# Who scales the raw expert weights in the weight preparation: GpSimd or ScalarE

## The reference

```python
# attention: 16 heads of 16, causal, only the 32 largest scores of each row kept
scores = where(causal, -inf, q @ k.T / 4); keep the top 32 of each row; softmax; @ v; @ Wo.T + bo
# experts: 8 experts, all computed for every token, weighted by a gate
h = relu(einsum('edi,bsi->bsed', proj_in, x))        # proj_in  8 x 512 x 256
o = einsum('eid,bsed->bsei', proj_out, h)            # proj_out 8 x 256 x 512
gate = einsum('bks,bkse->bse', weights, one_hot(ensembles, 8)); out = einsum('bsei,bse->bsi', o, gate)
# feed-forward: Hadamard transform, 4-bit activations, ternary weight
```

## Time and profile before

| | us |
|---|---|
| median of 3 runs | 622.53 |
| the profiled execution, its own time | 624.53 |
| its span in the trace | 622.7 |
| PE busy | 553.3 (89%) |
| DVE busy | 477.5 (77%) |
| ACT busy | 387.2 (62%) |
| POOL busy | 344.3 (55%) |
| DMA queue of the loads and stores | 9.6% of the 16 engines' span |

### The profile page before, as it was taken

The page is one execution under the profiler, slowest core; times in us unless marked ns, Lnnn a source line. Parts: engine busy times, 40 slices in busy tenths (PEclk is TensorE's granted clock), DMA queues, the critical chain, the costliest instruction groups (busy, mean ns, idle before and its releaser), DMA issues. The chain is left out here.

```text
span 622.7 us, 20334 instructions
## 1 busy us (share of the span) xinstructions
PE 553.3 (89%) x7156; PEld 478.9 (77%) x7156; DVE 477.5 (77%) x2995; ACT 387.2 (62%) x909; POOL 344.3 (55%) x336
## 2 busy tenths in 40 slices
PE   4565648999899999999999999999999999989942
PEld 3454537898788888888888888888888888878831
DVE  1898879986889978898879887988789898553213
ACT  3688558666567566766667576766575767646520
POOL 2488556753447464754556455655554656555831
PEclk9568578999999999999999999999999999999985
DMA  7244220001000200002000100020001000000000
GB/s 234 78 146 136 86 103 2 3 17 37 3 2 3 64 8 2 3 3 69 3 1 21 53 3 2 3 70 1 3 3 53 3 3 1 19 0 3 18 0 17
DMA packets 20021, 19.88 MB, mean 32 GB/s; under 512 B 1744, under 2 KB 17872, under 8 KB 19920
## 3 DMA queue, kind: packets, MB, share of 16 engines
q1 hardware_dynamic: 19920, 18.59, 9.6%
HBM read 16.49 MB, written 2.10 MB: 30 GB/s over the span
## 5 line engine op out<-in xcount | busy, mean ns | idle before, releaser
L462 POOL TENSOR_TENSOR h_lo<-h_raw,h_hi 128x512 f16<-128x512 f32 x128 | 149.5, 1169 | 158.9 <-ACT h_raw L580 158.2
L768 PE MATMUL ps_o<-w_hi,h_lo 128*128 128x256 f16 x512 | 139.8, 273 | 4.3 <-POOL h_lo L462 3.1
L752 PE MATMUL ps_z<-x1t_hi,w_lo 128*128 128x256 f16 x512 | 140.5, 274 | 0.6 <-DVE x1t_lo L910 0.6
L752 PE MATMUL ps_z<-x1t_lo,w_hi 128*128 128x256 f16 x512 | 140.3, 274 | 0.0
L752 PE MATMUL ps_z<-x1t_hi,w_hi 128*128 128x256 f16 x512 | 140.3, 274 | 0.0
L768 PE MATMUL ps_o<-w_hi,h_hi 128*128 128x256 f16 x512 | 139.5, 273 | 0.0
L768 PE MATMUL ps_o<-w_lo,h_hi 128*128 128x256 f16 x512 | 139.5, 273 | 0.0
L854 DVE MATCH_REPLACE8 taken<-next,taken 128x48 f32<-128x48 f32 (+2 forms) x576 | 127.6, 233 | 0.2
L576 ACT ACTIVATE h_hi<-ps_z 128x512 f16<-128x512 f32 x128 | 75.9, 593 | 57.9 <-PE ps_z L752 57.0
L849 DVE MAX8 next<-taken 128x8 f32<-128x48 f32 (+2 forms) x576 | 95.9, 235 | 0.1
L483 POOL TENSOR_TENSOR acc<-go_sb,acc 128x512 f32<-128x512 f32 x56 | 71.2, 1271 | 36.4 <-ACT go_sb L590 36.2
(11 more groups left out here) (106 smaller groups left out, 993.5 us busy)
## 6 DMA issues: line engine op xcount, KB each, us to landing
w_raw<-in_w1t SPq DMA_DIRECT2D x8, 512.0 KB, 3.8
w_raw<-in_w2t SPq DMA_DIRECT2D x8, 512.0 KB, 5.0
xt_sb<-in_xt SPq DMA_DIRECT2D x8, 256.0 KB, 3.3
x_sb<-in_x SPq DMA_DIRECT2D x8, 256.0 KB, 3.1
out<-out_sb SPq DMA_DIRECT2D x8, 256.0 KB, 2.1
ctx_sb<-in_ctx_w SPq DMA_DIRECT2D x8, 128.0 KB, 2.3
itok_sb<-in_itok SPq DMA_DIRECT2D x8, 128.0 KB, 2.5
wq_sb<-in_wqt SPq DMA_DIRECT2D x1, 256.0 KB, 2.9
```

Of the source, the lines that this page charges most:

```text
L462: nc.gpsimd.tensor_tensor(h_lo[:, e % 2, 2 * z:2 * z + 2, :], h_raw[:, z, :, :], h_hi[:, e % 2, 2 * z:2 * z + 2, :], ALU.subtract)\
L752: last = pe.matmul(ps_z[z][:, d * UT:(d + 1) * UT], w[:, e, c, at:at + P], x[:, c, :], start=n == 0, stop=n == len(terms) - 1)
L768: last = pe.matmul(ps_o[e % 2][:, b * D:(b + 1) * D], h[:, e % 2, c, b * SEQ:(b + 1) * SEQ], w[:, e, c, :], start=n == 0, stop=n == len(te ...
```

## The change

ACT makes the scaled raw array too: after each high part it runs a second activation over the same raw array, with the same scale, that writes the float32 result in place. The semaphore that GpSimd waits for is now raised by this second activation. GpSimd's scaling instruction and its wait are gone; its subtraction stays. For each expert ACT issues four 128x1024 activations instead of two, and GpSimd two instructions of that size instead of four. Nothing is moved in the order of the steps, and w2's high part now stands behind w1's scaling.

```diff
                 elif name in ("w1_low", "w2_low"):
                     e, = args
-                    i, raw, hi, lo, step_done, ready = (
-                        (0, w1_raw, w1_hi, w1_lo, w1_low_step, w1_low_ready) if name == "w1_low" else
-                        (1, w2_raw, w2_hi, w2_lo, w2_low_step, w2_low_ready))
+                    i, raw, hi, lo, ready = ((0, w1_raw, w1_hi, w1_lo, w1_low_ready) if name == "w1_low" else
+                                             (1, w2_raw, w2_hi, w2_lo, w2_low_ready))
                     pool.wait_ge(w_high_ready, 2 * e + i + 1)
-                    nc.gpsimd.tensor_scalar(raw[:, e % STAGED, :, :], raw[:, e % STAGED, :, :],
-                                            w_pow[:, e, i:i + 1], 1.0, ALU.mult, ALU.mult).then_inc(step_done, 1)
-                    pool.wait_ge(step_done, e + 1)
                     nc.gpsimd.tensor_tensor(lo[:, e, :, :], raw[:, e % STAGED, :, :], hi[:, e, :, :],
                                             ALU.subtract).then_inc(ready, 1)
...
                 elif name == "w_high":
                     e, = args
                     act.wait_ge(w_step, 3 * (e + 1))
-                    act.activation(w1_hi[:, e, :, :], w1_raw[:, e % STAGED, :, :], ACT.Copy,
-                                   scale=w_pow[:, e, 0:1]).then_inc(w_high_ready, 1)
-                    act.activation(w2_hi[:, e, :, :], w2_raw[:, e % STAGED, :, :], ACT.Copy,
-                                   scale=w_pow[:, e, 1:2]).then_inc(w_high_ready, 1)
+                    for i, (raw, hi) in enumerate(((w1_raw, w1_hi), (w2_raw, w2_hi))):
+                        act.activation(hi[:, e, :, :], raw[:, e % STAGED, :, :], ACT.Copy, scale=w_pow[:, e, i:i + 1])
+                        act.activation(raw[:, e % STAGED, :, :], raw[:, e % STAGED, :, :], ACT.Copy,
+                                       scale=w_pow[:, e, i:i + 1]).then_inc(w_high_ready, 1)
```

## The result

The changed kernel takes 630.07 us (median of 4 runs, 629.77 to 632.81) against 622.68 us before (4 runs): 7.4 us more. The profiled execution took 630.36 us with a span of 628.6 us, 5.8 and 5.9 us more than the one of before. Forecast were 6.4 more and 628.9 us.

What follows compares the result with a forecast made beforehand. PE bounds 200 to 580 us; before 94 us an engine-to-engine chain does. Terms 3.1 + 0 + 2.0 - 1.6 + 0.8 + 0.9 + 1.2 = 6.4 us on 622.53 give 628.9 us, range 624.9 to 631.4.

Steps and rivals of the forecast that it cites:

- Price of the added work: ACT's queue: each expert's two added float32 activations cost 2.1 us, bounds 0 and 2.3.
- Tile 0, 3.1: w_high 0 and 1 ahead of copy_scores and second copy_probs: keep 1.0 us late, attend and normalise 3.1 late.
- Tile 1, hidden: w_high 2: ACT's 2.03 us idle before the next copy hides the added 2.1; lateness stays 3.1.
- Tile 2, plus 2.0: w_high 3 straight before the exponentials that keep already waited for: no cover, plus 2.0, lateness 5.1.
- Tile 3, minus 1.6 plus 0.8: DVE's wait and slow small steps at w_scale(4) give back 1.6; w_high 4 makes keep wait 0.8; lateness 4.3.
- From keep of tile 3 to the first layer norm, lateness kept: Through turn_probs, copy_probs, attend and normalise the chain stays 4.3 us late; time won on DVE is worth nothing.
- w_high(5), costed at nothing: Expert 5's added activations hide in ACT's wait for PE's v product; uncovered they would cost 2.1 us.
- First layer norm, plus 0.9: ln1_apply's first DVE instruction is held by a subtraction, 2.1 us instead of 1.1; plus 0.9, lateness 5.2.
- Rival 1: Layer norm race goes otherwise: DVE slips in, 627.2 us, or w_high(6) is too late for POOL, 625.4; chance 0.22.
- Expert 7, plus 1.2: w_high 7 before exp(1|1): keep 1.2 us late, so PE's scores of tile 1|3 wait 1.2 more.
- Rival 3, the clock: Between 94 and 112 us PE's low-clock stretch is as long again: 2.0 us more, 630.9; chance 0.13.
- Rivals 2 and 4: 2: ACT's idle time hides everything, 622.5 us, chance 0.08. 4: the freed POOL/DVE port makes it faster, 619.1, chance 0.04.

Runs made afterwards that it cites:

- the kernel with expert 7 behind: Against the kernel before: ACT scales only expert 7, after exp and relu, and GpSimd's low parts of expert 7 move down its order; ratio 1.0013.
- the five experts: Against the kernel before: ACT's second, scaling activations only for experts 0, 1, 3, 4 and 7, GpSimd scaling the others; 630.16 us, ratio 1.0117.
- the single test: Against the kernel before: ACT's second, scaling activations only for experts 0 and 1, GpSimd scaling the others; ratio 1.0050, 3.1 us more.
- the fourth experiment: Kernel before plus one wait: GpSimd starts expert 6's low parts only when x1 is written, away from ln1_apply; 626.63 us, ratio 1.0071.
- the single ones: Three kernels against the one before: ACT scales only experts 0 and 1, only 3 and 4, or only 7; ratios 1.0050, 1.0056, 1.0026.
- the trace with expert 6 on ACT: Against the kernel before: ACT scales only expert 6, and GpSimd starts its low parts after the ternary weights are done; 621.72 us, ratio 0.9976.
- the one with the wait alone: Against the kernel before: GpSimd still scales every expert, but starts expert 6 only after the ternary weights are done; 626.77 us, ratio 1.0062.
- all scaling moved behind: Against the kernel before: all 16 scaling activations on ACT as a separate step, behind the exponentials or in an ACT wait; 638.01 us, ratio 1.0253.

## Why the prediction was right

The time lies in the forecast range, and the mechanism, place by place, was right up to tile 3. But that the sum fits so well is partly luck. Forecast were 6.4 us; measured are 7.4 by medians, 5.9 between the profiled executions and 8.4 (6.7 to 10.0) by the ratio of the runs, which leaves 6.4 just outside. In the two profiled executions errors of both signs cancel, and the reason is the clock during tile 3. The rows: PE's v product before, ACT's copy of v before and after, and the v product in the kernel with expert 7 behind, whose code is that of before up to there:

```profile
73.73 3.78 PE L645 MATMUL ps_misc<-wv_sb,xt_sb 128*128 128x256 f32 x8 [0.64 <-DVE o_sb L874]
...
77.55 0.60 ACT L525 ACTIVATE v_sb<-ps_misc 128x512 f32<-128x512 f32 x1 [2.99 <-PE ps_misc L645]
```

```profile
79.64 0.58 ACT L521 ACTIVATE v_sb<-ps_misc 128x512 f32<-128x512 f32 x1
```

```profile
73.93 2.00 PE L654 MATMUL ps_misc<-wv_sb,xt_sb 128*128 128x256 f32 x8 [0.64 <-DVE o_sb L883]
```

Seven traces have unchanged code up to here. Counted from the first w_squares, keep of tile 3 begins at 48.8 to 49.1 us in all of them. Then v takes 3.5 to 3.8 us in four (the kernel before among them) and 2.0 in three, and ln1_apply begins at 71.1 to 71.9 us in the first and 69.0 to 69.3 in the others. So traces have to be compared with traces of the same level. The changed kernel ran v at the upper level. All positions in us from the first w_squares:

| experts scaled by ACT | first w_squares at | keep of tile 3 | ln1_apply | first expert product | scores of 1\|3 | end of the span |
|---|---|---|---|---|---|---|
| *v at the lower level:* none (before) | 16.25 | 48.9 | 71.7 | 77.8 | 91.9 | 606.5 |
| 0, 1, 3, 4, 7 | 17.12 | 53.0 | 75.7 | 81.8 | 97.1 | 612.0 |
| 3, 4 | 17.02 | 50.0 | 72.7 | 78.8 | 92.9 | 607.4 |
| *v at the upper level:* 7, behind exp | 17.19 | 49.0 | 69.0 | 75.1 | 89.1 | 603.6 |
| 0, 1 | 15.85 | 51.8 | 72.2 | 78.3 | 92.4 | 606.9 |
| 2, 5, 6 | 16.42 | 48.8 | 70.8 | 77.6 | 91.1 | 605.6 |
| all (changed) | 15.56 | 53.5 | 74.6 | 81.5 | 97.1 | 613.0 |

At the lower level the five experts end 5.5 us later than the kernel before, which is the sum of the prediction's terms for them (6.4 less the 0.9 of the layer norm). At the upper level the changed kernel ends 9.4 us later than the one with expert 7 behind: 3 us more than forecast. This is one trace of each kernel, but the 8.4 us of the runs lie beside it. Term by term:

- **Price of the added work:** right, 1133 ns and a next start at 2 x 2.1 us. (Eight times 2.1 is 16.8, not 16.9; the sum doesn't use it.)
- **Tile 0, 3.1:** right. Keep waits 1.08 us for ACT at 28.25, normalise waits 3.11 instead of 1.03, and the single test gives 3.1 us by times and 3.2 by the table.
- **Tile 1, hidden:** right; keep of tile 1 shows no wait.
- **Tile 2, plus 2.0:** right, the keep's wait went from 0.52 to 2.49.
- **Tile 3, minus 1.6 plus 0.8:** nearly. w_scale(4) no longer waits and its small steps take 0.17 us; keep is 3.9 late, 4.6 counted from the first w_squares, against 4.3. Alone, experts 3 and 4 make keep 1.1 late and the end 0.9, where the terms give 1.2 (the expectation said 2.0, without the small steps). By times they cost 3.5 (2.1 to 4.9), and why that is more stays open.
- **From keep of tile 3 to the first layer norm, lateness kept:** right where the clock level is the same: 4.1 and 4.0 us with the five experts, 2.9 and 3.2 with experts 0 and 1. Between the two profiled executions it fell from 3.9 to 2.2 (90.19 against 87.98). PE ran attend and the v product of this tile in 1.11 and 1.99 us; before they took 1.90 and 3.78. The granted clock was 1.00 from 75.0 to 78.7 us against 0.50 from 71.0 to 77.5 before. Both levels occur with unchanged code, so the change need not be the reason.
- **w_high(5), costed at nothing:** this term failed. Its cover was ACT's wait for v, 2.99 us before, and with v at the upper level that wait is 0.31 us or none. In the changed kernel copy_v followed at 79.64 without idle time, and lateness against the upper level grew from 4.5 us at keep to 5.6 at ln1_apply. With experts 2, 5 and 6 alone it grew from nothing to 1.8. That can be most of the 1.8 us that this kernel lost by times.
- **First layer norm, plus 0.9:** right, 4.21 against 3.42. POOL's two subtractions ran from 90.01 for 4.24 us and each held one DVE instruction, the first from 90.19 for 2.08. The Trainium skill ("SBUF — State Buffer", section "SBUF: two separate sides") calls the shared port pair an exclusive lock for the whole instruction. The traces agree: 0.73 us once nothing of GpSimd runs beside the pair. Rival 1 didn't happen in any trace where GpSimd was free to start.
- **Expert 7, plus 1.2:** right alone (1.19 in PE's wait), too small in the changed kernel. There keep of 1|1 waited 2.07 us, DVE having been less late than ACT, and PE's wait grew to 3.02 us. After it the granted clock was 0.50 for 3.1 us (the row below, columns as in the earlier trace rows), so the scores took 2.20 us in place of 1.24 and the next products began at the lower level. From the first expert product to the end 2.9 us were added, not 1.2: 1.5 up to the scores, 1.4 behind them.
- **Rival 3, the clock:** it came true in part, beside the forecast and not in its place. From the scores to the end 514.4 to 514.6 us pass before and in seven other traces, 514.9 with the five experts, and 515.9 in the changed kernel. These 1.4 us go with the lower level after the longer wait; the rival had 2.0. At tile 3 the clock went the other way.
- **Rivals 2 and 4:** excluded by the result. Freeing the port alone brought nothing: the fourth experiment is slower than the kernel before.

```profile
112.70:115.80 3.10, 3.10 (x77) 2.74 (x78) 3.10 (x24) 0.90 (x2) 3.09 (x2) 0.50 0.00 0
```

So the cause is shown for the exposed places by the five-expert kernel and the single ones. Open are the size of expert 6's part in the times (only its 0.8 us in the trace is shown), what sets the clock level at tile 3, and in how many of the runs each level occurs.

## What to carry to other kernels

Work moved to an engine with 40% idle time costs what stands behind it in that engine's order: look for the consumer (here the exponentials for keep) and its slack, place by place, not at the share of busy time. A wait that hides work is good only as long as what it waits for is slow: here the cover of expert 5 went when PE's clock was up. Moving it behind the consumer helps only if its own product, here a staging buffer's release, has slack too. Before comparing two traces by position, look whether PE's clock was the same in the stretch between. When a held instruction is freed, ask what runs beside the holder next, and which wait was tied second.

## What the runs showed of the hardware

- With GpSimd instructions back to back, one VectorE instruction got through per GpSimd instruction: 3.42 us beside 1.12 and 2.12, 4.21 beside two of 2.1, 0.73 beside none.
- Even w_half, w_pow and w_inv, two to sixteen int32 elements per partition, are held: 0.95, 1.08 and 1.09 us in the trace with expert 6 on ACT against 0.17, w_pow 2.09 in the one with the wait alone and 2.04 and 2.05 in the one with all scaling moved behind.
- After a wait of 3.02 us PE came back at the lower clock level (0.50); after waits of 1.08 and 2.27 us the same matmuls took 1.24 us, so it had kept the upper one. After waits of 3.96 and 5.21 us in front of the first L2 its products took 0.42 us, after one of 1.77 us 0.27.
